# The place of one 128x512 VectorE addition in a software-pipelined GNN layer pair

## The reference

```python
def layer0(x, adj, W, b):                       # a graph convolution
    adj_hat = adj + eye(n)
    d = sum(adj_hat, -1) ** -0.5                # 0 where the degree is not positive
    agg = (d[:, None] * adj_hat * d[None, :]) @ x
    return relu(agg @ W.T + b)

h = maximum(layernorm(x), 0);  x = x + layer0(h, adj, W, b)
h = maximum(layernorm(x), 0);  x = x + layer1(h, adj, ...)
```

## Time and profile before

| what | value |
|---|---|
| time, median of 3 runs | 1775.73 us (1774.68 to 1776.88) |
| the profiled execution | 1775.3 us, its span 1773.5 us |
| TensorE busy | 1759.0 us, 99% |
| VectorE busy | 1201.8 us, 68% |
| ScalarE busy | 999.1 us, 56% |
| GpSimd busy | 817.5 us, 46% |
| chain that ended last | TensorE 96% |
| L497, all 64 | 99.7 us, 1559 ns each |

### The profile page before, as it was taken

How to read it: one execution, slowest core, us unless ns; L and a number is a source line. 1 busy time by engine, 2 the same in 40 slices (tenths; PEclk the granted TensorE clock), 3 DMA queues, 4 the chain that set the end, 5 groups by cost and what they waited for, 6 DMA issues and landing times.

```text
span 1773.5 us, 30896 instructions
## 1 busy us (share of the span) xinstructions
PE 1759.0 (99%) x10778; PEld 1557.3 (88%) x10778; DVE 1201.8 (68%) x2318; ACT 999.1 (56%) x1787; POOL 817.5 (46%) x988
## 2 busy tenths in 40 slices
PE   8999999999999999999999999999999999999998
PEld 7999999999999999999988888888888888888887
DVE  8999999999999956655764544544545545545445
ACT  6888888888888866666742333332333323333322
POOL 5788888888777637665731221211221212212211
PEclk9999999999999999999999999999999999999999
DMA  6567676766666554444674345444355453454442
GB/s 221 175 201 214 203 211 199 215 207 199 194 195 200 149 166 156 165 168 160 237 216 103 74 104 125 94 109 109 76 113 118 91 119 79 100 120 100 103 96 42
DMA packets 531865, 262.70 MB, mean 148 GB/s; under 512 B 366215, under 2 KB 494471, under 8 KB 531710
## 3 DMA queue, kind: packets, MB, share of 16 engines
q1 hardware_dynamic: 531166, 260.66, 53.5%
q10 hardware_dynamic: 544, 0.07, 0.0%
HBM read 151.58 MB, written 109.05 MB: 147 GB/s over the span
## 4 chain that ended last, share of the span: by engine, by line
PE 96%; DVE 1%; issue 1%; POOL 1%; DMA 1%; ACT 1%; SPq 0%; DVEq 0%; POOLq 0%; ACTq 0%
PE P L111 72%; PE P L614 6%; PE P L1021 4%; PE P L873 4%; PE P L643 4%; PE P L705 3%; PE P L662 1%; PE P L623 1%; DMA tt_w<-in_ttab 0%; POOL axl L577 0%; POOL af L574 0%; DVE sm L485 0%; DMA x<-in_x 0%; DVE sm L491 0%; DVE xct L1035 0%
## 5 line engine op out<-in xcount | busy, mean ns | idle before, releaser
L1000 POOL TENSOR_TENSOR xnx1l<-xnf,xnx1h 128x1024 fp32r<-128x1024 f32 x16 | 44.3, 2770 | 393.4 <-ACT xnx1h L993 393.4
L1000 POOL TENSOR_TENSOR xnx0l<-xnf,xnx0h 128x1024 fp32r<-128x1024 f32 x15 | 40.9, 2728 | 272.9 <-ACT xnx0h L993 272.9
L1126 ACT ACTIVATE nn<-gn,col 128x512 f32<-128x512 f32 x64 | 46.4, 725 | 193.4 <-DVE gn L1147 193.4
L1123 ACT ACTIVATE tr<-P,cold 128x512 f32<-128x512 f32 x64 | 44.2, 690 | 179.8 <-PE P L111 179.8
L1143 DVE SCALAR_TENSOR_TENSOR gn<-tr,gn 128x512 f32<-128x512 f32 x64 | 45.2, 706 | 137.4 <-ACT tr L1123 137.4
L574 POOL TENSOR_TENSOR af<-af,at 128x512 f32<-128x512 f32 x64 | 111.0, 1735 | 41.6 <-ACT af L365 40.1
L577 POOL TENSOR_TENSOR axl<-af,axh 128x512 fp32r<-128x512 f32 x64 | 102.3, 1599 | 54.7 <-ACT axh L383 54.7
L614 PE MATMUL P<-ah,hd 128*128 128x256 f32 x512 | 122.4, 383 | 0.5 <-ACT hd L399 0.5
L1156 DVE SCALAR_TENSOR_TENSOR tz<-tz,tr 128x512 f32<-128x512 f32 x63 | 43.6, 692 | 109.3 <-ACT tz L1137 109.2
L1137 ACT ACTIVATE tz<-P,cold 128x512 f32<-128x512 f32 x63 | 43.4, 689 | 123.2 <-PE P L111 123.2
L111 PE MATMUL P<-w1mh,xxh 128*128 128x512 f32 x256 | 106.6, 416 | 0.0
(11 more groups left out here) (214 smaller groups left out, 6403.0 us busy)
## 6 DMA issues: line engine op xcount, KB each, us to landing
xh_d<-xst SPq DMA_DIRECT2D x64, 320.0 KB, 4.8
y_d<-yo SPq DMA_DIRECT2D x80, 256.0 KB, 2.0
yt<-y_d SPq DMA_DIRECT2D x128, 160.0 KB, 4.5
xl<-xh_d SPq DMA_DIRECT2D x36, 512.0 KB, 4.4
x<-in_x SPq DMA_DIRECT2D x64, 256.0 KB, 2.7
a<-in_adj SPq DMA_DIRECT2D x64, 256.0 KB, 3.0
at<-in_adjt SPq DMA_DIRECT2D x64, 256.0 KB, 4.1
x_d<-x SPq DMA_DIRECT2D x64, 256.0 KB, 4.4
```

Source lines behind the costliest of these rows:

```text
L1000: e.e.tensor_tensor(o[1][:, :, :], xnf[p % 2][:, :, :, :].rearrange("p c i t -> p c (i t)"), o[0][:, :, :], ALU.subtract).then_inc(done, 1)
```

## The change

The step that adds the rectified output of layer 0 to the input (L497) moves on VectorE from behind the next input's statistics and degrees to directly behind L472, which writes what it reads. Its waits and its operands are the same.

```diff
--- before.py
+++ after.py
@@ -473,6 +473,13 @@
                         out=x2[b % 2][:, n, :], in0=P[OUT0][:, n * 256:n * 256 + 256], scalar=m[:, 30 + n:31 + n],
                         in1=b0[:, :], op0=ALU.mult, op1=ALU.add)
                 t.then_inc(S["u"], 1)
+            if live(i, 3):
+                b = i - 3
+                o = x2[b % 2]
+                e.wait_ge(S["u"], b + 1)
+                e.wait_ge(S[f"ldx{b % 2}"], loaded(b, 2))
+                e.e.scalar_tensor_tensor(out=o[:, :, :], in0=o[:, :, :], scalar=0.0, in1=xs[b % 5][:, :, :],
+                                         op0=ALU.max, op1=ALU.add).then_inc(S["x2"], 1)
             if live(i, 0):
                 b = i
                 m = sm[b % 7]
@@ -489,13 +496,6 @@
                 m = sm[b % 7]
                 e.wait_ge(S[f"lda{b % 2}"], loaded(b, 2))
                 e.e.tensor_reduce(m[:, 22:24], a_[b % 2][:, :, :], AX_X, ALU.add).then_inc(S["deg0"], 1)
-            if live(i, 3):
-                b = i - 3
-                o = x2[b % 2]
-                e.wait_ge(S["u"], b + 1)
-                e.wait_ge(S[f"ldx{b % 2}"], loaded(b, 2))
-                e.e.scalar_tensor_tensor(out=o[:, :, :], in0=o[:, :, :], scalar=0.0, in1=xs[b % 5][:, :, :],
-                                         op0=ALU.max, op1=ALU.add).then_inc(S["x2"], 1)
             if live(i, 0):
                 m = sm[i % 7]
                 e.wait_ge(S["deg0"], i + 1)
```

## The result

The changed kernel takes 1778.09 us (median of 22 runs, 1777.08 to 1779.06), the kernel before 1775.03 us (22 runs, 1774.24 to 1776.88). The ratio is 1.0016, interval 1.0010 to 1.0023: 3.06 us slower, within the 0.2% that I called no difference, and inside the range of 1773.8 to 1779.2. By the means of the same runs it is 2.91 us. The forecast was 1777.6. Its sum was +1.9 us on the median shown then, and +3.06 us was measured, so the place was right and the size was not. That 1777.6 lies only 0.5 us from 1778.09 is in part luck: the median of three runs that it started from was 0.7 us above that of the 22.

A forecast was written before the change was run, and what follows sets the result against it. TensorE's own work was taken to bound the later turns (0 us), VectorE the opening: 0.22 + 1.00 + 0.22 + 0.46 = +1.90 us on the median 1775.73 gave 1777.6 us, range 1773.8 to 1779.2.

The forecast's parts named there:

- What bounds the later turns: Later first-stage turns: TensorE's work alone fills 9.81 us, so freeing VectorE changes them by 0 us.
- the 0.07 us are a phase: Each turn: the 0.07 us from `agl` ready to TensorE's start is no price, as one late turn had 1.23 us slack.
- The waits on VectorE's own last result: L497 behind L472 and L502 behind L491 each wait 0.11 us more, together 0.22 us per turn.
- The turn before adds 0.22.: Opening: the turn ahead of the one near 39.7 us adds 0.22 us of waits to the forecast.
- Turn 6: Opening, near 39.7 us: L497 falls behind GpSimd's L574, +1.00; own waits +0.22; L508 behind L577 +0.46 us.
- L497's wait in the later turns: Later turns: L497 takes near 0.69 us without GpSimd's L568, up to 0.97 with it, in 37 turns.
- Rival (c): Every turn: L497 comes behind GpSimd's L574, VectorE's turn 1.28 us over TensorE's in 37 turns, about 1823 us; chance 0.05.

The follow-up runs named there:

- The extra instruction: One more VectorE reduction of 128x512 in turns 7 to 63: old order 1853.03 us against 1775.12 before; new order from turn 7 on 1774.77.
- between: Kernel before, but from turn 7 on the moved instruction stands between the input's statistics and its degrees: 1777.59 us against 1775.04, ratio 1.0015.

## Why the prediction was right or wrong

*What bounds the later turns: right.* The reading that the 0.07 us are a phase and that TensorE's own work fills 9.81 us came from one turn near the stage's end, and both the unchanged 9.813 us and the kernel with the new place in the later turns alone (1.0001) show it. The extra instruction shows the other half: there was also nothing behind those 0.07 us.

*The waits on VectorE's own last result: right in size, wrong in the number of turns.* The prediction put 0.11 us on each. The changed kernel has 0.90 from L472 to L481 (0.79 before) and 0.70 from L498 to L502 (0.59 before, from L491 to L497), and turns 3 to 5 each pay 0.24 to 0.26 us. The Trainium skill, "VectorE: DVE Perf Modes", section on the DRAIN, has a semaphore after each instruction as free. The prediction set its rows against that too simply: the kernel before sets these semaphores as well, and what costs 0.11 us here is the wait for the one set by the instruction directly in front.

*The step that failed* is the one on the opening: "The turn before adds 0.22." It took turn 5 alone as paying and put turns 3 and 4 at nothing without saying why. They pay as well, 0.26 + 0.25 us. In the profile of before something lay over each of them: in turn 3 VectorE waited 0.49 us for ScalarE's `agh`, with the clock low, and in turn 4 it waited 0.23 us, until 27.7, for the DMA that brings the tap table, and I took that as cover. In the execution with the old place in the opening VectorE reached that point at 27.98 and in the one with the new place at 28.52, and neither waited for the table. The cover comes and goes: of the six profiled executions with the old place in turns 3 and 4 and the table still in the opening, four waited for the table, 0.2 to 0.8 us, while none of the six with the new place did. The means of the runs, +0.74 and +0.78 us for turns 3 to 5, show little of it.

*Turn 6: right, with some luck.* The prediction had 1.68 us for the moved instruction, the trace 1.68; it had +1.68 for the turn (1.00 + 0.22 + 0.46) and the table above has +1.65. It rested on one row with a start 0.16 us behind GpSimd's, and the run "between" shows that a start 0.14 or even 0.5 us behind can also go first. One detail was another: not L508 fell into L577 but the small L502 ahead of it, 0.56 us instead of 0.17.

*Not in the sum at all:* the lower granted clock behind TensorE's 1.9 us of idle time, 1.5 us in the one profiled execution that shows it; by the times it is likely, not shown, that 10 of the 22 have it. With 0.26 + 0.25 + 0.24 + 1.65 = 2.40 us in an execution without cover, and 10/22 of 1.5 us, the mean should grow by 3.1 us; it grew by 2.91, and by 2.26 in the run with the idle time filled. That the two medians of the changed kernel differ (1778.09 and 1777.28) goes with the number of executions in the upper group (10 of 22, 2 of 11).

*L497's wait in the later turns: right without L568, too careful with it.* All 59 instances from 60 us on take 0.69 us, in the 37 turns with L568 as well, where the prediction chose 0.97. The Trainium skill, "SBUF — State Buffer", section "Who interferes with whom", has a two-input VectorE instruction contend with any GpSimd instruction that reads SBUF; beside L574 and L577 the rows agree, beside L568, which has one SBUF tensor as input, they do not.

*Rival (c)* was tried in its mild form only, between the statistics and the degrees, and its rule of who goes first didn't hold there. The extra instruction in the old order shows, however, that such a price is real: a VectorE queue that slips behind GpSimd's cost 1.4 us in each turn, where (c) had 1.28.

*Left open:* the kernels here, the one before too, have times in two groups about 0.8 us apart (before: 20 of 33 at 1774.4 to 1775.1, 13 at 1775.3 to 1776.0 in one set). The granted clock in the first 30 us differs among the profiled executions, and so does the wait for the tap table, but nothing was run to tie either to the groups. Nor is it shown what decides, behind the same idle time, whether the clock falls.

## What to carry to other kernels

An order that frees one engine in the steady turns does nothing for the time where another one fills them, and its price may lie in the few turns of the opening, where the queues stand otherwise; work those through one by one, and don't count a wait seen in one execution as cover. Where the bounding engine's next input is ready only just in time, one small instruction in each turn can cost more than twice its length each time (77.9 us for 57 times 0.6), so slack that costs 0.15% may be worth having if more work is to come, and the old order can be kept for the opening turns. An idle time of TensorE can cost more than its length, as in the one execution where 3.4 us at the lower clock followed 1.85 us of it and cost 1.5 us more.

## What the runs showed of the hardware

- A VectorE `tensor_scalar` on two float32 columns waits for a GpSimd instruction with two SBUF inputs to end: 1.27 us instead of 0.15, and 0.56 instead of 0.17.
- A two-input VectorE instruction beside GpSimd's one-input `tensor_scalar` doesn't wait: 0.69 us in all 37 turns.
- A VectorE instruction that waits for the semaphore set by the one directly in front starts 0.11 us later than one that doesn't (0.90 against 0.79 us, 0.70 against 0.59).
- Of two that start 0.14 to 0.16 us apart, GpSimd's first, in one place GpSimd went first (VectorE 1.68 us) and in another VectorE (0.67, GpSimd 1.98 instead of 1.37). VectorE went first even when it started 0.5 us later (0.67, GpSimd 2.35), and not when it started 0.39 us later in another order (1.66).
- Behind 1.85 us of idle time TensorE's granted clock was at its lower level for 3.4 us in one profiled execution, and behind 1.88 to 1.89 us at the full one in three others.
